# Four graph-attention layers on one core: two single-head products made of three passes of rounded high and low parts

## The reference

```python
h = jnp.maximum(_layernorm(x, axis=-1), 0.0)
x = x + gnn_ref(h, adj, ...)        # four different gnn_refs
```

```python
attn = jax.nn.softmax(scores, axis=-1)
return jnp.einsum('bij,bjh->bih', attn, node_features)
```

## Time and profile before

| | |
|---|---|
| median of 3 runs | 3080.85 us (3079.93 to 3082.12) |
| the profiled execution, its own time | 3083.84 us |
| its span, first to last instruction | 3082.1 us |
| granted TensorE clock, mean | 0.977 of full |
| PE busy | 2976.9 us, 97% |
| PEld busy | 2746.1 us, 89% |
| DVE busy | 2480.0 us, 80% |
| ACT busy | 2319.9 us, 75% |
| POOL busy | 2263.2 us, 73% |
| DMA queue q1 | 350.66 MB, 34.8% of 16 engines |

### The profile page before, as it was taken

One profiled execution on the slowest core, in us unless ns is written; L12 is line 12 of the kernel. 1 busy time (PEld: TensorE's weight loads), 2 busy tenths in 40 slices (PEclk: granted clock), 3 DMA queues, 4 the chain that ended last, 5 costly groups with the idle time before them and its releaser, 6 DMA issues. The chain is left out here.

```text
span 3082.1 us, 79166 instructions
## 1 busy us (share of the span) xinstructions
PE 2976.9 (97%) x21040; PEld 2746.1 (89%) x21040; DVE 2480.0 (80%) x8101; ACT 2319.9 (75%) x6433; POOL 2263.2 (73%) x3214
## 2 busy tenths in 40 slices
PE   7899999999999999999999999999999999999974
PEld 5789999999999999999999999999999999999964
DVE  3578888888888888888888888888888888888852
ACT  2567787778877788777787778877788777787752
POOL 3467777777777777777777777777777777777753
PEclk6999999999999999999999999999999999999985
DMA  5123333333333333333333333333333333333332
GB/s 195 34 69 123 117 119 122 108 124 118 119 123 106 125 117 119 122 109 122 118 119 121 108 122 120 120 118 112 121 120 119 118 110 122 120 120 119 96 107 93
DMA packets 205558, 355.71 MB, mean 115 GB/s; under 512 B 51904, under 2 KB 117568, under 8 KB 188736
## 3 DMA queue, kind: packets, MB, share of 16 engines
q1 hardware_dynamic: 205120, 350.66, 34.8%
HBM read 314.93 MB, written 35.59 MB: 114 GB/s over the span
## 5 line engine op out<-in xcount | busy, mean ns | idle before, releaser
L1454 POOL TENSOR_SCALAR rs<-mv,rs 128x1 f32<-128x1 f32 x512 | 357.6, 698 | 109.2 <-POOL rs L1451 108.8
L997 ACT ACTIVATE eT<-eT,tc 128x128 f32<-128x128 f32 x1024 | 314.1, 389 | 161.3 <-POOL eT L1534 161.3
L432 PE MATMUL bank_b<-w_hi,hT_hi 128*128 128x344 f32 x1536 | 419.8, 328 | 5.6 <-DVE g L1277 3.8
L432 PE MATMUL bank_c<-w_hi,g_hi 128*128 128x258 f32 x2048 | 414.1, 283 | 4.7 <-DVE x L1204 4.7
L432 PE MATMUL bank_c<-w_lo,g_hi 128*128 128x258 f32 x2048 | 414.5, 284 | 0.0
L432 PE MATMUL bank_b<-w_lo,hT_hi 128*128 128x344 f32 x1536 | 408.2, 320 | 0.0
L1329 DVE CUSTOM_DVE_ANT_0 t_all_L<-t_all_L,mask 128x128 f32<-128x128 f32 x1024 | 368.6, 413 | 27.0 <-DMA t_all_L<-t_dram_L 26.5
L432 PE MATMUL bank_b<-w_hi,hT_lo 128*128 128x344 f32 x1536 | 357.0, 327 | 0.0
L432 PE MATMUL bank_c<-w_hi,g_lo 128*128 128x258 f32 x2048 | 351.8, 284 | 0.0
L432 PE MATMUL bank_e<-w_hi,hT_hi 128*128 128x264 f32 x1024 | 341.1, 347 | 5.5 <-DVE out_sb L1372 5.4
L1540 POOL TENSOR_TENSOR eT<-eT,shift_all 128x512 f32<-128x512 f32 x256 | 331.1, 1294 | 4.6 <-ACT eT L997 4.4
(11 more groups left out here) (158 smaller groups left out, 8577.5 us busy)
## 6 DMA issues: line engine op xcount, KB each, us to landing
shift_all<-shift_dram SPq DMA_DIRECT2D x128, 1024.0 KB, 5.3
t_all_L<-t_dram_L SPq DMA_DIRECT2D x128, 512.0 KB, 3.7
x_in<-in_x SPq DMA_DIRECT2D x128, 256.0 KB, 2.6
t_all_L1a<-t_dram_L1a SPq DMA_DIRECT2D x128, 256.0 KB, 3.2
out<-out_sb SPq DMA_DIRECT2D x128, 256.0 KB, 3.1
t_all_L<-t_dram_L SPq DMA_DIRECT2D x256, 64.0 KB, 3.1
adj_in<-in_adj SPq DMA_DIRECT2D x128, 64.0 KB, 3.0
t_dram_L1a<-t_rows_L1a SPq DMA_DIRECT2D x512, 0.5 KB
```

The source lines that it names most:

```text
L432: last = mm(bank[:, 0:width], a[:, c * P:(c + 1) * P], w[:, c, b * width:(b + 1) * width], start=(first and c == chunks[0] and n == 0), st ...
L997: last = activation(eT[:, k, :], eT[:, k, :], ACT.Prelu, bias=tc3[:, k:k + 1], alpha=SLOPE)
L1454: ts(b, mv[layer][:, 0:1], r, -1.0, ALU.mult, ALU.mult).then_inc(sem(f"rs_made{layer}"), 1)
```

## The change

- `product_L1b` and `product_L2` are each three `F32R` matmuls (`product_of_parts`) where there was one float32 matmul. The layer-0 product stays as it is.
- ACT gets two more 128x512 copies per graph (`v_hi_L1b`, `v_hi_L2`), and `pT_L1b` and `pT_L2` now write `F32R`.
- DVE gets `v_lo_L1b` (128x512, both inputs in SBUF) and `pT_lo_L1b`, `pT_lo_L2` (128x128, one input in PSUM). POOL gets `v_lo_L2` (128x512).
- To make room in SBUF, `p1` shares the tensor of `e1`, `product` has two slots and not four, and the ring of output tiles has one slot and not two.
- SKEW is 11 and not 12, and the order of the calls in a step is another one on every engine.

```diff
@@ sizes and tensors
-SKEW = 12
+SKEW = 11
-        XR, MR, LR, TR, X1R, X2R, X3R, OR = 3, 10, 8, 4, 3, 2, 4, 2
+        XR, MR, LR, TR, X1R, X2R, X3R, OR = 3, 10, 8, 4, 3, 2, 4, 1
-        product = sb("product", [P, 4, D], BF16)
+        product = sb("product", [P, 2, D], BF16)
-        p1 = {k: sb(f"p_{k}", [P, P]) for k in one}
-        pT1 = {k: sb(f"pT_{k}", [P, P]) for k in one}
+        p1 = e1
+        split = ("L1b", "L2")
+        pT1 = {k: sb(f"pT_{k}", [P, P], F32R if k in split else F32) for k in one}
+        pT1_lo = {k: sb(f"pT_lo_{k}", [P, P], F32R) for k in split}
+        v_hi = {k: sb(f"v_hi_{k}", [P, D], F32R) for k in split}
+        v_lo = {k: sb(f"v_lo_{k}", [P, D], F32R) for k in split}
@@ PE
+            def product_of_parts(key, bank):
+                for n, (a, v) in enumerate(((pT1[key], v_hi[key]), (pT1[key], v_lo[key]), (pT1_lo[key], v_hi[key]))):
+                    last = mm(bank, a[:], v[:], start=(n == 0), stop=(n == 2))
+                last.then_inc(sem(f"{key}_out"), 1)
             def product_L2(t, g):
-                    pe.wait_ge(sem("L2_pT"), g.made())
+                    pe.wait_ge(sem("L2_pT_lo"), g.made())
+                    pe.wait_ge(sem("L2_v_lo"), g.made())
...
-                    mm(bank_a[:], pT1["L2"][:], h[2][:], start=True, stop=True).then_inc(sem("L2_out"), 1)
+                    product_of_parts("L2", bank_a[:])
@@ ACT
+            def v_hi_L1b(g):
+                    act.wait_ge(sem("xl2_made"), g.made())
+                    act.wait_ge(sem("L1b_out"), g.made(1))
+                    activation(v_hi["L1b"][:], xl2[:, 0:D], ACT.Copy).then_inc(sem("L1b_v_hi"), 1)
@@ DVE
+            def pT_lo_L1b(g):
+                    tt(pT1_lo["L1b"][:], bank_c[:, 0, 0:P], pT1["L1b"][:].bitcast(F32), ALU.subtract).then_inc(sem("L1b_pT_lo"), 1)
+            def v_lo_L1b(g):
+                    tt(v_lo["L1b"][:], xl2[:, 0:D], v_hi["L1b"][:].bitcast(F32), ALU.subtract).then_inc(sem("L1b_v_lo"), 1)
@@ POOL
+            def v_lo_L2(g):
+                    tt(v_lo["L2"][:], h[2][:], v_hi["L2"][:].bitcast(F32), ALU.subtract).then_inc(sem("L2_v_lo"), 1)
@@ order of a step on PE (from project_L1a_last on)
                 project_L3_last_high(t, t.graph(9))
+                project_L3_last_low(t, t.graph(9))
                 product_L2(t, t.graph(7))
-                project_L3_last_low(t, t.graph(9))
                 project_L1a_high(t, t.graph(3))
                 turn_exp_L1b(t, t.graph(5))
+                project_L1a_low(t, t.graph(3))
+                turn_mask_L3(t, t.graph(9))
+                product_L1b(t, t.graph(5))
                 turn_exp_L0(t, t.later_graph(2))
...
@@ order of a step on ACT (its middle, as it is now)
+                leaky_L1b(t.graph(5))
+                norm_2(t.graph(6))
+                exp_L1b(t.graph(5))
+                norm_3(t.graph(8))
+                pT_L1b(t.graph(5))
```

More of the change, by code:

```diff
@@ L368, in _ @@
                 send_L3(t.graph(9))
+                store(t.graph(11))
+                spread_L3(t.graph(9))
                 send_L2(t.graph(6))
-                spread_L3(t.graph(9))
             for s in range(OR):
@@ L831, in norm_2 @@
                         chunk_ready(act, ALL - 1)
-                    norm(2, g, x2[:, g.slot(X2R), :], "L2_out")
+                    act.wait_ge(sem("st_made2"), g.made(1))
+                    norm(2, g, x2[:, g.slot(X2R), :], "L2_v_lo")
             def norm_3(g):
@@ L1413, in _ @@
                 moments_2(t.graph(6))
-                values_L1b(t.graph(5))
                 hT_lo_L3(t.graph(9))
+                rows_L0(t.later_graph(2))
                 hT_lo_L1a(t.graph(3))
                 most_L2(t.graph(7))
+                values_L1b(t.graph(5))
+                stats_0(t.later_graph(0))
                 recip_L3(t.graph(11))
                 result_L3(t.graph(11))
+                recip_L2(t.graph(7))
+                rows_L1a(t.graph(3))
                 elu_L1a_first(t.graph(4))
-                rows_L1a(t.graph(3))
+                pT_lo_L2(t.graph(7))
                 elu_L1a_last(t.graph(4))
-                most_L0(t.later_graph(2))
-                recip_L2(t.graph(7))
-                residual_L2(t.graph(7))
-                rows_L3(t.graph(9))
-                most_L1b(t.graph(5))
-                moments_0(t.later_graph(1))
+                v_lo_L1b(t.graph(5))
+                g_lo_first(t.graph(4))
+                most_L1b(t.graph(5))
+                rows_L3(t.graph(9))
+                residual_L2(t.graph(7))
+                columns_L2(t.graph(6))
+                pT_lo_L1b(t.graph(5))
+                most_L0(t.later_graph(2))
                 stats_3(t.graph(7))
-                recip_L0(t.later_graph(2))
-                columns_L2(t.graph(6))
-                g_lo_first(t.graph(4))
-                rows_L2(t.graph(6))
                 recip_L1b(t.graph(5))
@@ L1579, in _ @@
                 scale_3(t.graph(8))
[L1580 removed]
                 scale_2(t.graph(6))
[L1582 removed]
+                v_lo_L2(t.graph(7))
+                make_mask(t.later_graph(2))
                 out_L3(t.graph(11))
+                scale_0(t.later_graph(1))
+                make_mask_loop(t.graph(2))
                 masked_L1b(t.graph(5))
                 g_lo_last(t.graph(4))
[L1586 to L1587 removed]
+                masked_L0(t.later_graph(2))
                 masked_L3_last(t.graph(10))
                 masked_L3_first(t.graph(10))
+                masked_L1a(t.graph(3))
+                shift_L3_last(t.graph(10))
 _INS = ["x", "adj", "L0_gnn_W", "L0_gnn_a1", "L0_gnn_a2", "L1_gnn_W1", "L1_gnn_b1", "L1_gnn_W2", "L1_gnn_b2",
```

151 lines of the change are left out of this document (88 added, 63 removed).

## The result

The changed kernel takes 3210.2 us (median of 4 runs, 3206.8 to 3215.7) against 3080.5 us of the kernel before in the same job: ratio 1.042, interval 1.040 to 1.044. It is slower by 130 us; 51 us slower had been predicted, so the direction held and the size did not, and the time lies beyond the range's end of 3180.

The account below looks back on a forecast made before the run. PE was taken as the bound: a 22.67 us step, less 0.35 saved, plus 0.82 of waits, is 23.14; over the execution +96 less 45 is +51, giving 3132 us against the median, 1.7% slower, range 3034 to 3180.

Parts of the forecast that it names:

- the collision: On POOL, scale_0's third instruction is held through v_lo_L1b and g_lo_first on DVE, ending 0.95 us late.
- the sum of the waits: PE's waits before turn_exp_L1b and the first L1b product: 0.82 us a step, bounds 0 and 1.92.
- Wrong: ... or a PE wait at another line, such as `turn_exp_L0`: Sign against the forecast: PE waiting somewhere other than before turn_exp_L1b and the first L1b product.
- The chain to exp_L1b: From PE's L3 product through POOL and ACT: exp_L1b ready at 8.31, so PE waits 0.64 us every full step.
- The wait before product_L1b: columns_L2 on DVE meets masked_L0 on POOL, pT_lo_L1b comes late, and PE waits 0.18 us more.
- PE's saving: Three fp32r passes of 0.228 us replace 0.86: 0.35 us a graph, 45 us in all; 22.32 a step with nothing late.
- Filling and draining ... 0 with 10 us either way: Start and end of the execution, bound by chains of waits in another order: no change, within 10 us.
- "nothing" for SKEW 11: SKEW 11 drops only a step that held one store, so it costs or gains nothing.
- PE stays the bound: Rival: the other engines' waits hide and PE's saving shows, 3036 us; chance 0.30.
- the engines' sums: Busy time a step rises to 20.4 us on DVE, 18.8 POOL, 19.2 ACT; none reaches 22.3.
- DVE late: Rival: columns_L2 loses a turn to masked_L3_last, waits are 1.92 us a step, 3261 us; chance 0.08.
- the turn: Whether POOL gets in between the two DVE subtractions: trace says no, wait 0.64 us; page's rule says yes, 0.75.

Follow-up runs that it names:

- e2: Changed kernel with one line moved: SyncE issues spread_L0 (64 KB) ahead of spread_shift_L3 (1 MB); 3155.9 us, ratio 1.025.
- e10: Changed kernel's order with the split undone (float32 products) and spread_L0 ahead of spread_shift_L3; 3084.6 us, ratio 1.000.
- e5: Changed kernel with the split undone and its order kept: float32 products, no added copies or subtractions; 3158.9 us, ratio 1.025.
- e4: Changed kernel with v_lo_L1b and g_lo_first each reading one input from PSUM instead of SBUF (values differ); 3134.8 us, ratio 1.018.
- e13: Changed kernel with spread_L0 ahead of spread_shift_L3 and, on POOL, scale_0 moved ahead of out_L3; 3066.9 us, ratio 0.995.
- e8: Kernel before with the split and smaller buffers, SKEW 12, g_lo_first behind recip_L2 and pT_lo_L1b behind rows_L2 on DVE; 3086.2 us, ratio 1.001.
- e14: e8 with targets_L3 also moved ahead of most_L3_first on DVE; 3086.8 us, ratio 1.001.
- e9: e2 with DVE reordered: v_lo_L1b behind most_L1b, then pT_lo_L1b, then columns_L2; 3400.9 us, ratio 1.105.
- e1: Changed kernel with masked_L1b moved on POOL right behind out_L3, ahead of scale_0 and make_mask_loop; 3335.2 us, ratio 1.083.

## Why the prediction was right and wrong

The direction came out right, and not by luck: the collision that the prediction described is there, and with the DMA order mended (e2) the kernel is still 2.5% slower. That kernel, at 3155.9 us, is the one that the prediction worked out; its own range was 3105 to 3165.

- **The step that failed** is the sum of the waits, "I take 0.82". They are 23.82 - 22.18 = 1.64 us in the mean. In a short step they are 1.25: 0.64 before `turn_exp_L1b`, 0.28 before the first product of L1b, and 0.33 that the prediction put at nothing, 0.20 before `turn_exp_L0` and 0.13 before `product_L0`. The steps in which the copy of `spread_L0` comes later still add 0.39 in the mean, at all three places. e2 takes away most of this 0.39, and 0.22 of the second wait, and leaves the 0.33. The prediction took SyncE's order up only for the store and let `masked_L0` start without waiting for its copy. e2 gives 54 us for this, e10 against e5 gives 74. The sentence "Wrong: ... or a PE wait at another line, such as `turn_exp_L0`" named the sign, but no term of the sum stood for it.
- **The chain to exp_L1b** held to a hundredth: 0.65 us measured for 0.64, with L1514 at 1.21 and the pair on DVE as described. e4 and e13, which take it away in two ways, bear it out.
- **The wait before product_L1b** was 0.28 in a short step for 0.18. `columns_L2` did meet `masked_L0`, as described, but a `masked_L0` that was late by its copy.
- **PE's saving** was nearly right. The passes start 0.23 us apart, 0.68 for three. In the same order the shortest steps of 1000 to 2000 us are 22.47 us with float32 (e10) and 22.19 split (e13): 0.28, where 0.35 had been said. But PE's list was started from too high: the changed order with float32 products is 22.47 and not 22.67, so with nothing late the step is 22.18, not 22.32. This hid 0.14 us a step of the missing wait, and that the forecast was not further off is luck.
- **"Filling and draining ... 0 with 10 us either way"** held: +3 and -12. So did "nothing" for SKEW 11. Both kernels run the last `out_L3` in the same step, the 139th, and end 3.7 or 3.8 us after it. The draining is shorter in the new order, with the same number of steps: 206 us in the changed kernel, 201 in e10, 203 in e13, against 217 before and 219 to 220 in e8 and e14. Which move does it was not tried. It is also most of what makes e13 faster: its 116 steps take 2626.7 us for 2630.5, its draining 203 for 217.
- **The rivals.** "PE stays the bound" rested on the engines' sums. They do fit, and e13, with PE busy 99.3%, comes near to it; but in e8 and e14, with DVE 90% busy, tenths were lost at other places. "DVE late" did not occur in the changed kernel; e9 is that rival in kind, with 2.0 us for the 1.92 that I had bounded it with, though before `turn_exp_L0`.
- Of the Trainium skill ("SBUF — State Buffer", Who interferes with whom) the rule on pairs held in e4. On the turn, the changed kernel agrees with 0.65, not the 0.75 that the page's rule would give.

## What to carry to other kernels

Where calls move, walk every engine's list, the one that issues the DMAs first: a 64 KB copy put behind a 1 MB one cost 54 us with the split and 74 without it, not much less than the collision that had been foreseen (75, e4). A wait found is not the sum of waits; after each, ask for every operand that PE takes in the step when it is asked for and when it is ready. And in a kernel whose engines are 77 to 99.8% busy a move of 0.3 us can cost 1.3%: try a moved call alone, before giving a gain or a loss to the edit that came with it.

## What the runs showed of the hardware that was not expected

- A copy of 64 KB issued 0.9 us behind one of 1 MB on the same queue let its reader start 7.7 us after the issue in the step shown, and one issued 0.5 us ahead of it landed after 4.7 us in the median; with 0.9 us of head start it had been 3.1.
- A small POOL instruction with its operands in SBUF was held through two DVE instructions in a row that read two SBUF inputs each (1.21 us), for 0.69 where there was one (e9), and not at all where both read one input from PSUM (0.27, e4). In e13 `mask_loop` on POOL, begun 0.22 us after the first of the same pair, took 0.87 and ended while the second, lengthened to 0.91, was under way. What decides whether POOL gets in was not tried.
- In two places where "issue" stood as the releaser of a POOL instruction that reads a tile filled by DMA, the wait fits a copy that had not landed (changed kernel, e1); in the changed kernel it went when the copy was issued sooner (e2).
- Waits of 2 to 3 us of PE in nearly every step (e9) went with falls of the granted clock to half, 3.4 us each; in the full steps of the changed kernel, which waits 0.5 us at `turn_exp_L1b` in most of them, there was none.
